# Value-row loads, graph 3's row copies and graph 2's list ranks at other places of the order

## The chip, the cores and the metric

One core of a Trainium2 chip runs the whole program. The metric is the device time of one launch in microseconds (us). The kernel before took 1257.94 us, median of 3 runs (1255.73 to 1259.4).

## What is computed

Eight graphs of 1024 nodes with 128 features, and an adjacency matrix of 1024 x 1024 each (about 8 neighbours a row), go through two layers with residuals:

```python
h = jnp.maximum(_layernorm(x, axis=-1), 0.0)
x = x + _L0_gnn_ref(adj, h, L0_gnn_W, L0_gnn_b)
h = jnp.maximum(_layernorm(x, axis=-1), 0.0)
x = x + _L1_gnn_ref(h, adj, ...)
```

The first layer takes for each node the first 25 neighbours, the maximum over their feature rows, and a linear layer with ReLU of [node, maximum]. The second is a transformer block with 8 heads of 16: scores masked by adjacency in either direction and the diagonal, softmax, output projection, layer norm, a feed-forward net of 512, layer norm.

## The kernel before, in words

The program is written engine by engine, with semaphores set by hand. Time is cut into slots s = -3 to 8 of 32 steps n (`STEPS`). In slot s, TensorE and ScalarE do the attention of graph g = s: step n is one tile of 128 keys for a group of four heads and one half of the queries (`scores`, L1664 and L1668; `exps`, L1460; `contexts` of the step before, L1684). Steps 0 to 15 take the near half of the queries, 16 to 31 the far half. What belongs to other graphs hangs on numbered steps, by tables at the head of the file: the end of graph p = s - 1 (projection, feed-forward, output), the first layer of graph f = s + 1, the neighbour lists of graph r = s + 2, the adjacency and rows of graph l = s + 3. The three engines TensorE, ScalarE and SP issue strictly in this order; a wait of one instruction holds all behind it.

The pieces that the change and the prediction name:

- Lists. DVE reads the adjacency tiles (`list_tile`, L825 and L829), takes candidates, and `merge_pair` makes 25 keys per node. `find_crowded` (L853, L854) tells whether any block of 128 columns held more than it kept. TensorE turns that vector into a row (L1845, at `full_at` of `RANK_AT`), `crowded_tiles` (L859) reads it, `make_lists` (L881 to L900) counts and signals the matmuls `rank_counts` (L1608 to L1611, at `counts_at`), and `list_ranks` (L906 to L909) makes the ranks. POOL waits for them in `scatter_lists` (L667), reloads the sorted lists (`load_lists`, L660) and then gathers neighbour rows, one indirect DMA for each list position (`gather_tile`, L694), some of them held to a pace of the score steps.
- Maxima. DVE reduces the gathered rows (`pool_tile`, L1015), POOL sends them out sorted back (`send`, L674), SP loads them as `ag`, and TensorE transposes them (L1570, at the first of `aggregate_steps`: 22 for f = 1, 20 for f > 1). ScalarE copies the halves out (L1440), and the linear layer follows (L1565 to L1772).
- Banks. PSUM tile `m` has three banks that all of this shares. `refill(bank)` makes TensorE wait until its last user is done. Bank 2 holds the edge counts of step 20 (`NEAR_AT_1`, entry `20: [(2, 2)]`, matmuls L1593 to L1598), and before them the context rows that step 18 transposed (L1713), until DVE's `context` (L1031, L1034) has normalised them.
- Graph 3's rows. `first_norm` on DVE makes the factors, ScalarE's `first_norm` (L1476) applies them to `xh` in eight copies at steps of `H_AT_1`, SP stores them (`store_h_rows`, L502) and loads graph 4's later.
- Value rows. ScalarE writes them at step 30 (L1497); SP spreads them over `va` in seven pieces per head group (`turn_values`, L485 and L487), of which the contexts of the next slot's first step need those of group 0. SP's `load_list_tile` waits until the buffer's last tile has been read:

```python
if i >= 2:
    sp.wait_ge(s_adj_used, i - 1)
sp.dma_start(adj_t[:, t % 2, :], adj[l, t * P:(t + 1) * P, :]).then_inc(ADJ[t % 2], 16)
```

The DVE order in slot 0, written out by hand in `first_slot`, has at the place in question:

```python
find_crowded()
merge_pair(6)
wide_maxima(0, 1)
context(0, 1)
crowded_tiles(2)
make_lists(2)
list_ranks(2)
join_first(1)
first_norm(3)
linear(1)
```

Of the kernel before, what the change touches and what calls it, by code (L numbers as in the profile page):

```python
# [64 lines left out]
NEAR_AT_1 = {17: [(0, 2), (1, 0)], 20: [(2, 2)], 21: [(3, 2)], 23: [(4, 2)], 24: [(5, 2)], 25: [(6, 2)], 31: [(7, 2)]}  # L65
H_AT = {17: (0, 2), 19: (2, 4), 21: (4, 5), 22: (5, 8)}
H_AT_1 = {22: (0, 4), 23: (4, 8)}

CTXT_AT, EARLY_CTXT_AT = [{3}, {3}], {20}
OUTPROJ_AT, EARLY_OUTPROJ_AT = [{4}, {5}], {21}  # L70
# [16 lines left out]

RANK_AT = {0: (-2, 3, 7, 8), 1: (0, 0, 2, 4), 2: (0, 19, 21, None), 3: (1, 11, 12, None)}  # L90


def rank_bank(r):
# [14 lines left out]
def masks_at(s):  # L108

    return MASK_AT_FRONT.get(s, {}) if s < 0 else (MASK_AT_0, MASK_AT_1, MASK_AT)[min(s, 2)]  # L110
# [7 lines left out]
def rank_steps(r):  # L118

    return RANK_AT.get(r, (r - 2, 3, 7, None))  # L120

# [67 lines left out]
def program(nc, x, adj, L0_W, L0_b, Wqkv, bqkv, Wo, bo, ln1_g, ln1_b, W1, b1, W2, b2, ln2_g, ln2_b, out):  # L189
# [6 lines left out]
    with ctx:  # L196
# [199 lines left out]
        def live(g):  # L396
            return 0 <= g < B
# [55 lines left out]
        with nc.Block() as block:  # L453

            @block.sync
            def _(sp):

                def load_list_tile(l, t):
                    i = l * T + t
# [4 lines that stand above are left out]
                def load_shift(g, qh):  # L464

                    sp.wait_ge(s_nflag, g + 1)
                    wide = sp.value_load(nflag_i[0:1, g % 2:g % 2 + 1], min_val=0, max_val=1)
                    with sp.If(wide > 0):
                        sp.wait_ge(s_gshift, 4 * g + 2 * qh + 2)
                        for h in range(HEADS):  # L470
                            q = queries_of(h // GROUP, g, qh)
                            at = h % GROUP * SPAN + (D - first_row(h) % SPAN)
                            sp.dma_start(q[at:at + 1, :], shf[h * TH:(h + 1) * TH, :]).then_inc(s_shift_in, 16)
                    with sp.Else():
                        sp.sem_inc(s_shift_in, 16 * HEADS)

                def turn_values(f, hg):

                    sp.wait_ge(s_v_sb, 2 * f + 2)
                    if f:  # L480
                        sp.wait_ge(s_pv, STEPS * f - (0 if hg else T))
                    for a in range(GROUP):
                        at = a * SPAN
                        h = hg * GROUP + a
                        sp.dma_start(va[0:P - at, hg, a, :, :], v_rows[at:P, h, :, :]).then_inc(VA[hg], 16)  # L485
                        if a:
                            sp.dma_start(va[P - at:P, hg, a, :, :], v_rows[0:at, h, :, :]).then_inc(VA[hg], 16)  # L487
# [10 lines left out]
                def store_h_rows(l):  # L498
                    sp.wait_ge(s_h_ready, T * (l + 1))
                    if l == 0:  # L500
                        sp.wait_ge(s_h_rows_out, 16)
                    sp.dma_start(rows_of(table(l)), xh[:, :, :]).then_inc(s_h_rows_out, 16)  # L502

                def load_x1_half(f, h):

                    k = slice(h * TH, (h + 1) * TH)
                    sp.dma_start(x1[:, f % 2, k, :], graph(x, f)[:, k, :]).then_inc(s_x1_in, 16)

                def load_x(l):
                    if l:  # L510
                        sp.wait_ge(s_h_rows_out, 16 * (l + 1))
                    sp.dma_start(xh[:, :, :], graph(x, l)).then_inc(s_x_in, 16)

                def load_h(f):
                    if f:
                        sp.wait_ge(s_hT_ready, 2 * f)
                    else:
                        sp.wait_ge(s_h_rows_out, 32)
                    sp.dma_start(hl[:, :, :], rows_of(table(f))).then_inc(s_hl_in, 16)

                def load_pooled(f):
                    sent(f + 1)
                    sp.wait_ge(s_aT_ready, 2 * f)
                    sp.dma_start(ag[:, :, :], rows_of(pooled[f % 2])).then_inc(s_ag_in, 16)
# [24 lines left out]
                def first_slot():  # L549
                    load_shift(0, 0)  # L550
                    turn_values(0, 1)
                    load_list_tile(2, 2)
                    load_list_tile(2, 3)
                    store_h_rows(2)
                    load_list_tile(2, 4)
                    load_h(1)
                    load_list_tile(2, 5)
                    load_x1_half(1, 0)
                    load_list_tile(2, 6)
                    load_x1_half(1, 1)  # L560
                    load_list_tile(2, 7)
                    load_x(3)
                    load_list_tile(3, 0)
                    load_list_tile(3, 1)
                    load_pooled(1)
                    load_shift(0, 1)
                    store_h_rows(3)
                    for t in range(2, 6):
                        load_list_tile(3, t)
                    turn_values(1, 0)  # L570

                prologue()
                first_slot()
                for s in range(1, B + 1):
                    g, p, f, r, l = s, s - 1, s + 1, s + 2, s + 3
# [820 lines left out]
            def _(act):  # L1396
# [109 lines left out]
                for s in range(-3, B + 1):  # L1506
                    g, p, f, r, l = s, s - 1, s + 1, s + 2, s + 3
                    for n in range(STEPS):
                        if live(g):
                            exps(g, n)  # L1510
                        if n == 0 and live(p):
                            context_out(p, 3)
                        if n in (8, 16, 24) and live(g):
                            context_out(g, n // T - 1)
                        if live(g):
                            for kt, bank in (FAR_AT if g else FAR_AT_0).get(n, ()):
                                bar(g, kt, bank, 1, s_far_counts, s_far_ready)
                        for e, h, _ in closing(s, n, CTXT_AT, EARLY_CTXT_AT):
                            half_out(turned[:, h * HALF:(h + 1) * HALF], h, s_ctxT_ready, 2 * e + h + 1, s_ctxT_sb)
                        for e, h, _ in closing(s, n, NT_AT, EARLY_NT_AT):  # L1520
                            norm_out(e, h)
                        for e, h, at in closing(s, n, HID_AT, EARLY_HID_AT):
                            for k, bank in at[n]:
                                hidden(e, h * FC + k, bank)
                        for ahead, t in masks_at(s).get(n, ()):
                            if live(s + ahead):
                                mask_tile(s + ahead, t)
                        if s == -2 and n == 10:
                            for kt, bank in NEAR_0:
                                bar(0, kt, bank, 0, s_near_counts, s_near_ready)  # L1530
                        if s == 0 and n in (7, 8):
                            for t in range((n - 7) * TH, (n - 6) * TH):
                                first_norm(2, t)
                        if live(l) and l not in (0, 2):
                            for t in range(*(H_AT if l > 4 else H_AT_1).get(n, (0, 0))):
                                first_norm(l, t)
                        if live(f):
                            if n in (18, 19) if f else n in (3, 4):
                                h = n - (18 if f else 3)
                                half_out(hT[:, h * HALF:(h + 1) * HALF], 0, s_hT_ready, 2 * f + h + 1, s_hT_sb)  # L1540
                            for kt, bank in near_at(f).get(n, ()):
                                bar(f, kt, bank, 0, s_near_counts, s_near_ready)
                            if n == aggregate_steps(f)[0]:
                                halves_out(aT, f, s_aT_ready, s_aT_sb)
                            if n == aggregate_steps(f)[2]:
                                if p >= 0:

                                    act.wait_ge(s_out_stored, 32 * (p + 1))
                                halves_out(h2T, f, s_h2T_ready, s_h2T_sb, ACT.Relu)
                            if n == 30:  # L1550
                                value_rows(f, 0)
                                value_rows(f, 1)
                            for j, bank in projections_at(f).get(n, ()):
                                projection(f, j, bank)
# [367 lines left out]
```

## Time and profile before

| | |
|---|---|
| median of 3 runs | 1257.94 us (1255.73 to 1259.4) |
| profiled execution, its own time | 1255.8 us |
| its span | 1253.8 us, 29308 instructions |
| granted TensorE clock, mean | 0.943 |
| busy: TensorE, DVE, ScalarE, POOL | 83%, 64%, 64%, 59% |

Times in the rows are microseconds from the start of the span. L numbers are lines of the kernel before. A row of a timeline gives start, duration, engine, line, operation, out<-in, shapes and count; in brackets stands how long the engine was idle before it, and what ended that. Slot 0 runs from about 160 to 295 us, slot 1 to 458.

### The profile page before, as it was taken

The numbers are of one execution on the slowest core, as the hardware profiler recorded it, in microseconds if no ns is written. First come the engines' busy times: TensorE is split into PE (matmuls) and PEld (weight loads), VectorE is DVE, ScalarE is ACT, GpSimd is POOL, SyncE is SP. The second block draws the span as 40 slices with busy tenths as digits, with TensorE's granted clock in tenths as the row PEclk, the third lists the DMA queues.
The fourth block names the chain that finished last, engine by engine and source line by source line (L and its number), as shares of the span: only waits on it lengthen the run. The fifth ranks groups of instructions, "written<-read, shape, count | busy, mean of one in ns | idle before, by whom it ended". The sixth has DMA issues, their size and how long they took to land.

```text
span 1253.8 us, 29308 instructions
## 1 busy us (share of the span) xinstructions
PE 1043.9 (83%) x11014; PEld 405.0 (32%) x11014; DVE 797.5 (64%) x3053; ACT 805.7 (64%) x1031; POOL 737.4 (59%) x741
## 2 busy tenths in 40 slices
PE   0125587688984989999999999999999999999874
PEld 0112331233331334343434333433343334333222
DVE  7856877767788477977797769776363534122323
ACT  1321257677852867788778877887678756875541
POOL 4776677567777777777777777776777520000000
PEclk9567889899996999999999999999999999999996
DMA  6533336426423433453345334431242110000000
GB/s 188 167 67 107 104 94 160 145 70 140 119 67 113 110 111 106 123 105 104 110 127 105 100 114 126 104 93 52 80 70 71 53 52 18 21 1 10 10 9 8
DMA packets 95156, 110.77 MB, mean 88 GB/s; under 512 B 17080, under 2 KB 75968, under 8 KB 94976
## 3 DMA queue, kind: packets, MB, share of 16 engines
q1 hardware_dynamic: 68352, 62.67, 16.4%
q0 software_dynamic: 22816, 44.61, 15.5%
q8 instruction: 101, 1.65, 0.6%
q10 hardware_dynamic: 3808, 1.19, 0.4%
q14 instruction: 79, 0.65, 0.2%
HBM read 91.10 MB, written 12.85 MB: 83 GB/s over the span
## 4 chain that ended last, share of the span: by engine, by line
PE 64%; ACT 11%; DVE 7%; POOL 7%; issue 6%; DMA 3%; SPq 0%; DVEq 0%; POOLq 0%; ACTq 0%
PE sc L1664 20%; PE cb L1684 13%; ACT probs L1460 10%; PE sc L1668 7%; PE m L1741 5%; PE m L1749 5%; POOL nb_low L716 3%; PE m L1570 3%; POOL nb_low L694 2%; PE m L1593 2%; DMA nb_low<-h_rows,lsorted 1%; PE m L1723 1%; PE m L1598 1%; PE m L1792 1%; PE m L1771 1%
## 5 line engine op out<-in xcount | busy, mean ns | idle before, releaser
L1460 ACT ACTIVATE probs<-sc 128x1024 f32<-128x1024 f32 x512 | 496.7, 1023 | 245.8 <-PE sc L1668 242.4
L694 POOL DMA_INDIRECT nb_low<-h_rows,lsorted x474 | 470.3, 992 | 168.8 <-issue 129.1
L1684 PE MATMUL cb<-probs,va 128*17 128x512 f32 x2048 | 270.6, 600 | 4.1 <-issue 3.2
L1664 PE MATMUL sc<-q_near,k_g 32*128 32x512 f32 x1024 | 147.8, 647 | 21.4 <-ACT probs L1460 17.2
L1664 PE MATMUL sc<-q_far,k_g 32*128 32x512 f32 x1024 | 149.6, 654 | 16.9 <-ACT probs L1460 15.8
L1015 DVE TENSOR_REDUCE agg<-nb_low 128x128 f32<-128x1024 f32 (+10 forms) x58 | 96.3, 1660 | 60.2 <-DMA nb_low<-h_rows,lsorted 34.4
L1668 PE MATMUL sc<-barred,negident 32*32 32x512 bf16 x4096 | 112.5, 386 | 1.8 <-issue 1.8
L829 DVE MAX8 cand<-keys 128x8 f16<-128x128 f16 x512 | 105.3, 278 | 2.2
L716 POOL DMA_INDIRECT nb_low<-h_rows,first_lists x80 | 80.5, 1006 | 41.9 <-issue 22.5
L1668 PEld LDWEIGHTS sc<-barred,negident 32*32 32x32 bf16 x4096 | 35.4, 88 | 200.8 <-issue 200.8
L1452 ACT ACTIVATE barred<-m 128x512 bf16<-128x512 f32 x128 | 72.9, 608 | 39.5 <-PE m L1598 39.5
L1471 ACT ACTIVATE m<-keys 128x1024 fp8e5<-128x1024 f16 x64 | 67.1, 1058 | 38.3 <-DVE keys L825 38.3
L825 DVE SCALAR_TENSOR_TENSOR keys<-adj_t,prio 128x1024 f16<-128x1024 int32 x64 | 79.0, 1234 | 10.5 <-DVEq L1022 7.7
L674 POOL DMA_INDIRECT pooled_rows<-agg,lsorted x56 | 60.6, 1082 | 26.4 <-issue 14.6
L667 POOL DMA_INDIRECT neighbour_lists<-lst,rank_i x48 | 49.5, 1031 | 28.8 <-DVE rank_i L909 15.3
L1741 PE MATMUL m<-turned,w1T 128*128 128x512 f32 x128 | 65.2, 634 | 1.0 <-ACT turned L1444 1.0
L1749 PE MATMUL m<-wide_tiles,w2T 128*128 128x512 f32 x128 | 63.2, 617 | 0.0
L1664 PEld LDWEIGHTS sc<-q_near,k_g 32*128 32x128 f32 x1024 | 40.4, 184 | 70.4 <-ACT probs L1460 43.6
L1664 PEld LDWEIGHTS sc<-q_far,k_g 32*128 32x128 f32 x1024 | 40.8, 186 | 65.0 <-ACT probs L1460 44.3
L694 POOL DMA_INDIRECT nb_high<-h_rows,lsorted x46 | 46.5, 1011 | 14.0 <-issue 12.8
L1684 PEld LDWEIGHTS cb<-probs,va 128*17 128x17 f32 x2048 | 34.1, 95 | 62.6 <-issue 61.9
L1484 ACT ACTIVATE wide_tiles<-m,b1c 128x512 f32<-128x512 f32 x64 | 44.0, 687 | 15.2 <-PE m L1741 13.7
(180 smaller groups left out, 1442.2 us busy)
## 6 DMA issues: line engine op xcount, KB each, us to landing
adj_t<-in_adj_dram SPq DMA_DIRECT2D x64, 512.0 KB
nb_low<-h_rows,lsorted POOLq DMA_INDIRECT x474
xh<-in_x_dram SPq DMA_DIRECT2D x8, 512.0 KB
h_rows<-xh SPq DMA_DIRECT2D x8, 512.0 KB
hl<-h_rows SPq DMA_DIRECT2D x8, 512.0 KB
x<-in_x_dram SPq DMA_DIRECT2D x16, 256.0 KB
out_dram<-h2T SPq DMA_DIRECT2D x16, 256.0 KB, 3.2
ag<-pooled_rows SPq DMA_DIRECT2D x7, 512.0 KB
```

What stands on the lines that cost most here:

```text
L694: pool.indirect_dma_start(out=dst, out_offset=None, in_=h_rows[0:(f + 1) * (N + 1), :], in_offset=bass.IndirectOffsetOnAxis(ap=lsorted[:, ...
L716: pool.indirect_dma_start(out=first_slots(t)[:, k, :], out_offset=None, in_=h_rows[0:(f + 1) * (N + 1), :], in_offset=bass.IndirectOffsetO ...
L825: nc.vector.scalar_tensor_tensor(out=keys[:, t, :], in0=adj_t[:, t % 2, :], scalar=0.0, in1=prio[:, :], op0=ALU.not_equal, op1=ALU.mult).t ...
L829: ch.step(nc.vector.max(cand[:, t, 8 * c:8 * c + 8], keys[:, t, c * CW:(c + 1) * CW]))
L1015: ch.link(nc.vector.tensor_reduce(a, first.rearrange("p k c -> p c k"), AX.X, ALU.max))
L1452: nc.scalar.activation(barred[:, kt, half * HALF:(half + 1) * HALF], m[:, bank, :], ACT.Relu, bias=1.0, scale=-1.0).then_inc(done, 1)
L1460: nc.scalar.activation(probs[:, i % 2, 2 * pair:2 * pair + 2, :], sc[:, 2 * pair:2 * pair + 2, :], ACT.Exp, scale=SCALE).then_inc(s_probs, 1)
L1664: nc.tensor.matmul(sc[:, a, :], k[part, :], q[part, :], start=True, stop=False)
L1668: last = nc.tensor.matmul(sc[c * SPAN:(c + 1) * SPAN, a, :], negident[b, b], barred[b, kt, qh * HALF:(qh + 1) * HALF], start=False, stop=True)
L1684: last = nc.tensor.matmul(cb[a * SPAN:a * SPAN + VW, :], va[:, u % 2, a, kt, :], probs[:, i % 2, a, :], start=(kt == 0), stop=(kt == T - 1))
L1741: nc.tensor.matmul(m[:, bank, :], w1T[:, k * P:(k + 1) * P], turned[:, half * HALF:(half + 1) * HALF], start=True, stop=True).then_inc(s_h ...
L1749: last = nc.tensor.matmul(m[:, half, :], w2T[:, k, :], hid[:, k, :], start=(k == 0), stop=(k == FC - 1))
```

## The change

Three edits of order; no operation is added or removed, and no semaphore count changes.

```diff
+H_AT_3 = {24: (0, 4), 25: (4, 8)}
...
-RANK_AT = {0: (-2, 3, 7, 8), 1: (0, 0, 2, 4), 2: (0, 19, 21, None), 3: (1, 11, 12, None)}
+RANK_AT = {0: (-2, 3, 7, 8), 1: (0, 0, 2, 4), 2: (0, 21, 22, None), 3: (1, 11, 12, None)}
...
-                    for t in range(2, 6):
+                    for t in range(2, 5):
                         load_list_tile(3, t)
                     turn_values(1, 0)
+                    load_list_tile(3, 5)
...
-                            for t in range(*(H_AT if l > 4 else H_AT_1).get(n, (0, 0))):
+                            for t in range(*(H_AT if l > 4 else H_AT_3 if l == 3 else H_AT_1).get(n, (0, 0))):
                                 first_norm(l, t)
```

The numbers of `RANK_AT` are slot, step of the crowded-rows transpose, step of the counts, step of the sort. Graph 3 is l in slot 0 alone, so all three edits act in slot 0. `H_AT_1` has steps 22 and 23 for these rows.

TensorE's order, from the head transposes of step 18 (`hl`) to the start of the counts, before:

```order
L1570 MATMUL m<-identf,hl 128x128 x4
L1664 MATMUL sc<-q_far,k_g 128x512 x4
L1668 MATMUL sc<-barred,negident 32x512 x16
L1684 MATMUL cb<-probs,va 17x512 x4
L1845 MATMUL m<-identf,full 1x128
L1570 MATMUL m<-identf,hl 128x128 x4
L1664 MATMUL sc<-q_far,k_g 128x512 x4
L1668 MATMUL sc<-barred,negident 32x512 x16
L1684 MATMUL cb<-probs,va 17x512 x4
L1593 MATMUL m<-m,ident 128x512
L1596 MATMUL m<-ident 128x128
L1598 MATMUL m<-ident,m 128x128 x4
```

The same place now (all lines are two further down), to the crowded-rows transpose of step 21:

```order
L1572 MATMUL m<-identf,hl 128x128 x4
L1666 MATMUL sc<-q_far,k_g 128x512 x4
L1670 MATMUL sc<-barred,negident 32x512 x16
L1686 MATMUL cb<-probs,va 17x512 x4
L1595 MATMUL m<-m,ident 128x512
L1598 MATMUL m<-ident 128x128
L1600 MATMUL m<-ident,m 128x128 x4
L1666 MATMUL sc<-q_far,k_g 128x512 x4
L1670 MATMUL sc<-barred,negident 32x512 x16
L1686 MATMUL cb<-probs,va 17x512 x4
L1847 MATMUL m<-identf,full 1x128
```

The first row here is the transposes of step 19. The crowded-rows transpose stood ahead of them; it now stands behind the edge count of step 20 (the L1595 row) and the scores and contexts of step 21. The counts, which stood behind step 21's contexts, stand behind step 22's.

## Rows read from the trace of the kernel before

**Rows 1.** The page: the chain that ended last, shares of the span by engine

```profile
PE 64%; ACT 11%; DVE 7%; POOL 7%; issue 6%; DMA 3%; SPq 0%; DVEq 0%; POOLq 0%; ACTq 0%
```

**Rows 2.** Windows: us; busy (x count) of PE, PEld, DVE, ACT, POOL; clock; DMA; GB/s

```profile
160.00:295.00 135.00, 110.52 (x1378) 41.25 (x1378) 100.59 (x419) 95.57 (x125) 92.49 (x89) 0.95 0.42 116
295.00:458.00 163.00, 131.57 (x1363) 50.29 (x1363) 119.26 (x445) 102.60 (x132) 124.62 (x124) 0.92 0.40 108
458.00:585.00 127.00, 124.24 (x1375) 47.92 (x1371) 97.45 (x371) 100.28 (x128) 96.95 (x95) 1.00 0.42 111
...
241.40:246.00 4.60, 4.56 (x38) 1.63 (x38) 3.21 (x24) 1.45 (x2) 0.68 (x1) 0.64 0.10 35
```

**Rows 3.** Timeline of PE in slot 0, steps 19 to 24

```profile
232.00 1.14 PE L1664 MATMUL sc<-q_far,k_g 32*128 32x512 f32 x8 [0.23 <-ACT probs L1460]
...
241.44 0.37 PE L1845 MATMUL m<-identf,full 128*1 128x128 f32 x1 [6.95 <-DVE full L854]
...
242.60 2.09 PE L1664 MATMUL sc<-q_far,k_g 32*128 32x512 f32 x8
...
245.99 0.39 PE L1593 MATMUL m<-m,ident 128*128 128x512 fp8e5 x1
...
247.14 1.14 PE L1664 MATMUL sc<-q_far,k_g 32*128 32x512 f32 x8 [0.48 <-ACT probs L1460]
...
249.56 0.19 PE L1608 MATMUL m<-abovesum,onesb 128*128 128x26 bf16 x1
...
260.33 0.39 PE L1565 MATMUL m<-bias_tiles,onesb 128*128 128x512 bf16 x1 [2.49 <-ACT wide_tiles L1440]
```

**Rows 4.** Timeline of DVE in slot 0, context rows and lists of graph 2

```profile
245.14 0.42 DVE L1034 TENSOR_TENSOR ctxn<-m,rden 128x256 f32<-128x256 f32 x1
245.48 0.27 DVE L859 TENSOR_REDUCE crowded<-m 1x1 f32<-1x128 f32 x1
...
249.19 0.18 DVE L888 CAST abovesum<-rprod 128x26 bf16<-128x26 f32 x1
```

**Rows 5.** Timeline of ACT in slot 0, steps 19, 22 and 26

```profile
233.55 1.94 ACT L1460 ACTIVATE probs<-sc 128x1024 f32<-128x1024 f32 x2 [1.12 <-PE sc L1668]
...
258.15 1.65 ACT L1476 ACTIVATE xh<-xh,nw 128x128 f32<-128x128 f32 x4 [3.40 <-DVE nw L790]
...
272.69 1.94 ACT L1460 ACTIVATE probs<-sc 128x1024 f32<-128x1024 f32 x2 [0.17 <-PE sc L1668]
```

**Rows 6.** Timeline of POOL, first scatter and first gather of graph 2

```profile
252.12 1.18 POOL L667 DMA_INDIRECT neighbour_lists<-lst,rank_i  x1 [10.04 <-DVE rank_i L909]
...
271.02 1.01 POOL L694 DMA_INDIRECT nb_low<-h_rows,lsorted  x1 [4.28 <-issue]
```

**Rows 7.** Waits of POOL, 271 to 393 us: total us, times, longest us

```profile
POOL nb_low L694 <- issue: 22.4, 61, 4.3
```

**Rows 8.** Timeline of DVE and of PE in slot 1

```profile
344.58 2.13 DVE L1015 TENSOR_REDUCE agg<-nb_low 128x128 f32<-128x1152 f32 x1 [2.97 <-DMA nb_low<-h_rows,lsorted]
...
348.32 0.27 PE L1845 MATMUL m<-identf,full 128*1 128x128 f32 x1 [2.01 <-DVE ctxn L1034]
...
348.63 0.28 DVE L859 TENSOR_REDUCE crowded<-m 1x1 f32<-1x128 f32 x1 [0.45 <-PE m L1845]
...
351.98 0.18 DVE L888 CAST abovesum<-rprod 128x26 bf16<-128x26 f32 x1
...
383.99 1.12 PE L1757 MATMUL m<-identf,turned 128*128 128x128 f32 x4 [9.19 <-DVE turned L1054]
...
405.09 1.97 PE L1570 MATMUL m<-identf,ag 128*128 128x128 f32 x8 [9.21 <-DMA ag<-pooled_rows]
```

**Rows 9.** Timeline of SP and of PE at the border to slot 1

```profile
276.85 16.71 SPq L462 DMA_DIRECT2D adj_t<-in_adj_dram  x4
293.66 1.21 SPq L485 DMA_DIRECT2D va<-v_rows  x2
...
303.43 1.91 PE L1684 MATMUL cb<-probs,va 128*17 128x512 f32 x8 [3.23 <-issue]
```

## The prediction

> **What bounds the kernel now.** I read the page's chain of waits first: it runs through TensorE for 64% of the span, with DVE and POOL at 7% each [rows 1]. The sum of busy times by stage says where to look [rows 2]: the third (458 to 585 us, the pattern of the later ones) takes about 127 us, TensorE 98% busy at the full clock of 2.4 GHz, while the first takes 135 us and the second 163 us, with POOL busy for 124.6 us of that. All three edits act in slot 0 and on the border to slot 1, so the question is what ends the waits there.
>
> Slot 0 first, on TensorE [rows 3]. Step 19 starts at 232.00. In it TensorE stands 6.95 us for the crowded-rows vector of graph 2, until 241.44 [rows 3]. Right after, the step's score matmuls take 2.09 instead of 1.14 us, and the stretch from 241.4 to 246.0 has a granted clock of 0.64 [rows 2]: most of it ran at 1.2 GHz, after an idle time of 7 us. The second stand, 2.49 us at 260.33, is for the copy of the pooled rows, which ScalarE runs behind the row copies of graph 3, and these wait 3.40 us for DVE's norm [rows 5].
>
> POOL next. It stands 10.04 us for graph 2's ranks, scatters the lists at 252.12, reloads them and gathers from 271.02 [rows 6]. From there to 371 us no gather waits more than 0.3 us, save the first: POOL is issue-bound for 100 us [rows 7]. What waits for it is slot 1: DVE waits 2.97 us for a gather until 344.58, TensorE then 2.01, 9.19 and 9.21 us, for DVE work behind those gathers and for the pooled rows [rows 8]. **So slot 1 is set by the moment at which the ranks of graph 2 are ready,** not by TensorE. After 458 us only TensorE and ScalarE are on the chain; a shift that stands there stays to the end.
>
> **Crowded rows and counts, from steps 19 and 21 to 21 and 22.** What the edit wants is the 6.95 us: steps 19 and 20 could run first. Step 19 needs 2.42 us from its first score to the end of its contexts (247.14 to 249.56), then half a microsecond of transposes; ScalarE ends its exponentials at 235.5 (233.55 and 1.94) [rows 5], step 20 starts there and is through at 238.0. But the next instruction in step 20 is the edge count of tile 2, in bank 2, which holds the context rows of step 18 until DVE has normalised them. DVE does that at 245.14 to 245.56 [rows 4], behind the crowded-rows reduction and a merge of lists, and nothing in its queue since the transposes of step 18 waits for TensorE. Before, the count began at 245.99 and waited for nothing. Now it begins at 245.6. **The stand moves from step 19 to step 20 and lasts 7.6 us; of 6.95 us some 0.4 us is won.**
>
> From there the new places cost. Step 21's scores and contexts now stand ahead of the crowded-rows transpose, and they run just behind a stand as long as that of before, so I take step 20's own times of before for them: 3.39 us from score to end of contexts (242.60 to 245.99), and about 1.0 us for the edge count in place of 0.6. Thus: count 245.6, step 21 at 246.6, transpose at 250.0. DVE takes it 0.31 us later, as at 348.32 and 348.63 in slot 1 [rows 8], and needs from there to the vector for the counts 3.53 us (348.63 to 352.16; where DVE came late to it, 245.48 to 249.37 [rows 4], it was 3.89). That gives 253.9, and step 22's contexts are through at 253.6 (exponentials of step 21 end at 251.1, plus 2.42). The counts start at 254.0 instead of 249.56: **+4.4 us**. With the full clock the same sum is 246.2, 248.6, 248.9, 252.5, counts at 252.7: +3.1 us, the lower end. With 3.89 in place of 3.53 it is +4.8. Behind the counts everything up to POOL is a fixed chain of 2.56 us (249.56 to 252.12), and from the first scatter to the first gather 18.9 us: scatter at 256.5, first gather at 275.4. POOL is past its pacing there (the first gather needs only step 24's scores), so nothing gives these back.
>
> On the clock, the Trainium skill, "TensorE: Matmul & The Clock Gate", section "What's actually happening", says that for modelling the ramp is under 1% of a typical span and that one should not fit a count of slow matmuls; by that the 1.3 us between my two sums would be left out and the result be the +3.1. The row of step 20, 2.09 against 1.14 us, speaks for keeping it.
>
> **Row copies of graph 3, from steps 22 and 23 to 24 and 25.** Removed: ScalarE's wait of 3.40 us for DVE's norm and 1.65 us of copies ahead of the pooled rows' copy, so TensorE's 2.49 us. But the join of graph 1, behind the ranks in DVE's queue, is now 4.4 us later too, and step 22's transposes wait for it. Of these 4.4 us the 2.49 and about 1 us of slack ahead of the transposes are taken off again, so I put step 24 about 1 us behind before. Added: 1.65 us in each of steps 24 and 25, and ScalarE has only 0.17 us idle at the end of step 25 [rows 5], which makes 1.5 us there; in step 24 the linear layer's matmuls hide a part, and I take half, 0.8 us (together 2.3, between 1.5 and 3.3). Together TensorE enters slot 1 some 3 us later. SP's store of these rows waits for the last of them, at the end of step 25, about 275 us by my estimate (step 26's exponentials, before at 272.69, stand behind them); the next tile load behind it was issued at 276.85 [rows 9] when its buffer came free, so a cover of 1 to 2 us stays, more with DVE late.
>
> **Value rows ahead of tile 5.** Before, SP's four tile loads end at 293.56, the last held by DVE's keys, and the seven pieces follow from 293.66 at 0.6 us or more each [rows 9]; TensorE stands 3.23 us for the last of them and does the contexts in 1.91 us [rows 9], about half of it at the full clock by my estimate: 3.23 and 0.9 make 4.1 us to be had. Now they are issued as soon as the value rows are written (some 3 us later than before, by the shift above) and no 512 KB tile is ahead of them. I take all of it as removed. Tile 5 is issued some 5 us later; DVE needs it behind the first tile of graph 2 and the tile before, over 10 us later than it was issued, so a part of that is left.
>
> **What comes of the sum.** TensorE is then about 1 us ahead of before at step 2 of slot 1 (+3 less 4.1). But the gathers are 4.4 us later: DVE's 344.58 becomes 349.0, TensorE's 348.32 becomes 352.7, and so on with 383.99 and 405.09. Gains on TensorE ahead of these only lengthen the stands. So copies and value rows are worth nothing now; what hides them is TensorE's own wait for the gathers. If that cover were gone they would be worth about 1 us together. The sum is +4.4 us on the profiled execution, 1255.8 us, which lies 2.1 us under the median of the runs: 1260.2 against it, **1262.3 us** against the median of 1257.94. A measurement of this kernel can tell about 0.3%, 3.8 us, from no change, so this is just beyond.
>
> **Rivals.** (a) The delay is real but smaller: full clock for step 21, +3.1 us, 1261.0, or a gather that lands sooner behind other loads. For it: the clock may return at another point of the step. Against: the rows after the stands at 241.44 and 303.43 are both slow. 22%. (b) The edit does not reach the path: context rows and ranks come so that the counts are ready by 249.6 to 251, POOL starts as before, and slot 1 hides all else: 1257.9. Against: bank 2 is free at 245.56 only. 12%. (c) **Faster:** slot 1 is not held by the gathers but by TensorE, that is, the landing at 344.58 has over 4.4 us of slack. It decides from the point where gathers land before DVE asks. Then the 3.23 us and the slow contexts (4.1 us) and the 2.49 us come through, less 2.3 us on ScalarE: -4.3 us, 1253.6. Against: DVE waits 2.97 us there and TensorE 20 us after it [rows 8]. 6%. (d) More than the sum: the longer stands of slot 1 (3 us and more at step 8, before the norm's transposes) bring the low clock into the feed-forward matmuls, whose results DVE needs; each such stretch costs 1 to 2 us: 1264 to 1267. 10%. The forecast has 50%.
>
> **Numbers.** The range reaches from (b) to the lower half of (d): 1257.0 to 1266.0. Beyond 1261.7 is slower by over 0.3%: the forecast's upper part, (d) and a third of (a), 0.58. Within: the rest of the forecast, most of (a), (b), 0.35. Faster: (c) and a little noise, 0.07.
>
> **What would show it.** In the new profile: no wait for the crowded rows in step 19, but an idle time of about 7.6 us on the edge count of step 20, ended by the context rows at 245.6; slow scores in step 21; counts at 254; first scatter at 256.5, first gather of graph 2 at 275.4; no wait of the step-1 contexts for the value rows; no wait for the pooled rows' copy at 260; DVE's wait for the gather ended at about 349, the transposes of the sum at 388.4, the pooled rows at 409.5; slots from the third on at 126 us. I am wrong if the scatter starts before 254, or if it starts at 256 and 405.09 has not moved with it.

## The result

The changed kernel takes **1263.54 us** (median of 13 runs, 1260.47 to 1265.26); the kernel before, in the same sessions, 1259.4 us (13 runs, 1255.67 to 1261.97). The ratio is 1.0035, 95% interval 1.0023 to 1.0047: 4.1 us slower between the medians, where +4.4 was the sum and 1262.3 the forecast (counted from the 1257.94 us of the first three runs).

The profiled execution of the change has a span of 1262.0 us, 8.2 more than the one before. Not all of this is the change's: DVE's context rows in slot 0, which no edit touches, end at 248.76 in place of 245.56. So 3.2 us lie ahead of the edits (2.1 of them already at the scores of step 18), and I compare distances from that point. Timeline of the change, TensorE in slot 0 and 1 (lines are two further down than in [rows 3] and [rows 8]):

```profile
248.91 0.59 PE L1595 MATMUL m<-m,ident 128*128 128x512 fp8e5 x1 [8.82 <-DVE ctxn L1036]
249.96 2.09 PE L1666 MATMUL sc<-q_far,k_g 32*128 32x512 f32 x8
...
253.33 0.27 PE L1847 MATMUL m<-identf,full 128*1 128x128 f32 x1
...
254.46 1.14 PE L1666 MATMUL sc<-q_far,k_g 32*128 32x512 f32 x8 [0.36 <-ACT probs L1462]
...
257.66 0.17 PE L1610 MATMUL m<-abovesum,onesb 128*128 128x26 bf16 x1 [0.72 <-DVE abovesum L890]
...
261.79 1.71 PE L1666 MATMUL sc<-q_far,k_g 32*128 32x512 f32 x8
...
266.23 0.38 PE L1567 MATMUL m<-bias_tiles,onesb 128*128 128x512 bf16 x1
...
308.99 1.05 PE L1686 MATMUL cb<-probs,va 128*17 128x512 f32 x8
...
357.74 0.34 PE L1847 MATMUL m<-identf,full 128*1 128x128 f32 x1 [2.06 <-DVE ctxn L1036]
...
393.43 1.11 PE L1759 MATMUL m<-identf,turned 128*128 128x128 f32 x4 [7.70 <-DVE turned L1056]
...
414.91 1.33 PE L1572 MATMUL m<-identf,ag 128*128 128x128 f32 x5 [8.99 <-DMA ag<-pooled_rows]
```

The stand of 6.95 us for the crowded rows [rows 3] is gone, and one of 8.82 us stands on the edge count of step 20, ended by DVE's context rows. The counts begin 8.9 us after these rows' end (257.66 less 248.76); before it was 4.0. The two small waits that the other edits aim at are gone: nothing is waited for at 266.23 (before 2.49 us) or at 308.99 (before 3.23 us [rows 9]). The waits of slot 1 are all there.

DVE in the same kernel, the timeline of its context rows, the crowded-rows reduction, the vector for the counts, and its wait for a gather in slot 1:

```profile
248.34 0.42 DVE L1036 TENSOR_TENSOR ctxn<-m,rden 128x256 f32<-128x256 f32 x1
...
253.64 0.28 DVE L861 TENSOR_REDUCE crowded<-m 1x1 f32<-1x128 f32 x1 [4.87 <-PE m L1847]
...
257.33 0.18 DVE L890 CAST abovesum<-rprod 128x26 bf16<-128x26 f32 x1
...
354.00 2.13 DVE L1017 TENSOR_REDUCE agg<-nb_low 128x128 f32<-128x1152 f32 x1 [2.73 <-DMA nb_low<-h_rows,lsorted]
```

POOL, the same timeline view, answers to [rows 6]:

```profile
260.22 1.17 POOL L669 DMA_INDIRECT neighbour_lists<-lst,rank_i  x1 [14.92 <-DVE rank_i L911]
...
275.42 0.95 POOL L662 DMA_DIRECT2D lsorted<-neighbour_lists  x1 [2.73 <-issue]
...
280.04 1.01 POOL L696 DMA_INDIRECT nb_low<-h_rows,lsorted  x1 [3.67 <-issue]
```

The first scatter waits 14.92 us for the ranks, 4.9 more. Less the 3.2 us, the first gather is 5.8 us late. The waits of slot 1 end at 354.00, 357.74, 393.43 and 414.91, 6.2, 6.2, 6.2 and 6.6 us late, where the forecast had 4.4 for all of them; at the end of the span it is 5.0. By stage (windows; columns as in [rows 2]), the third slot is what it was, 126.5 us against 127.0. The last line is the stretch behind the stand, with a granted clock of 0.66:

```profile
304.00:468.50 164.50, 134.21 (x1363) 49.99 (x1359) 120.08 (x446) 102.67 (x131) 125.89 (x124) 0.91 0.39 108
468.50:595.00 126.50, 124.99 (x1383) 48.08 (x1379) 96.80 (x370) 100.40 (x129) 96.50 (x94) 1.00 0.41 109
248.90:253.40 4.50, 4.49 (x39) 1.44 (x40) 0.00 (x0) 1.53 (x3) 0.00 (x0) 0.66 0.27 80
```

### The profile page after: what moved, and what is told of

It is laid out like the page before. It is cut to its first block, busy times and chain, and to the rows that moved or that the text cites. A ratio compares the mean times of both kernels' runs of the same rounds, so it can differ in the third digit from the quotient of the medians.

```text
span 1262.0 us, 29308 instructions
## 1 busy us (share of the span) xinstructions
PE 1055.2 (84%) x11014; PEld 407.7 (32%) x11014; DVE 797.9 (63%) x3053; ACT 806.4 (64%) x1031; POOL 736.5 (58%) x741
## 3 DMA queue, kind: packets, MB, share of 16 engines
q0 software_dynamic: 22816, 44.61, 15.4%
## 4 chain that ended last, share of the span: by engine, by line
PE 61%; DVE 12%; ACT 9%; POOL 6%; issue 6%; DMA 5%; DVEq 1%; SPq 0%; POOLq 0%; ACTq 0%
PE sc L1666 18%; PE cb L1686 13%; ACT probs L1462 7%; PE sc L1670 6%; PE m L1743 4%; PE m L1751 4%; POOL nb_low L718 3%; DMA nb_low<-h_rows,lsorted 3%; PE m L1572 3%; POOL nb_low L696 2%; DVE agg L1017 2%; PE m L1595 2%; PE sc L1708 2%; PE m L1600 1%; DVE st L769 1%
## 5 line engine op out<-in xcount | busy, mean ns | idle before, releaser
L1686 PE MATMUL cb<-probs,va 128*17 128x512 f32 x2048 | 273.5, 606 | 2.2 <-DMA va<-v_rows 1.6
L1670 PEld LDWEIGHTS sc<-barred,negident 32*32 32x32 bf16 x4096 | 35.4, 88 | 200.5 <-issue 200.5
L1595 PE MATMUL m<-m,ident 128*128 128x512 fp8e5 x128 | 52.2, 408 | 9.7 <-DVE ctxn L1036 8.8
```

Of the source, the lines that this page charges most:

```text
L1595: nc.tensor.matmul(o, ident8[:, :], m1[:, f % GRAPHS, kt, half * HALF:(half + 1) * HALF], start=True, stop=False)
L1670: last = nc.tensor.matmul(sc[c * SPAN:(c + 1) * SPAN, a, :], negident[b, b], barred[b, kt, qh * HALF:(qh + 1) * HALF], start=False, stop=True)
L1686: last = nc.tensor.matmul(cb[a * SPAN:a * SPAN + VW, :], va[:, u % 2, a, kt, :], probs[:, i % 2, a, :], start=(kt == 0), stop=(kt == T - 1))
```

## The experiments

Two theories stand against each other: slot 1 is held by the gathers, so the moment of graph 2's ranks decides; or it is held by TensorE, so what TensorE wins or loses in slot 0 decides. All ratios are to the kernel before, with 95% intervals, 12 runs of each kernel against 17 to 35 of the kernel before.

**1. The rank edit alone.**

```diff
-RANK_AT = {..., 2: (0, 19, 21, None), ...}
+RANK_AT = {..., 2: (0, 21, 22, None), ...}
```

> Only the crowded-rows transpose and the counts of graph 2 are moved (steps 21 and 22). Theory (ranks late, slot 1 held by the gathers): all of the 4.1 us is here, ratio 1.003 to 1.004; TensorE stands 7 to 9 us on the edge count of step 20 until DVE has normalised the context rows, the counts start 4 to 5 us later against the end of that normalisation than before (4.0 us after it before, 8.8 in the change), the first scatter likewise. Rival (the row copies of steps 24 and 25 do it, 2 to 3 us of ScalarE, and the ranks little): ratio under 1.0015.

Measured: 1.0029 (1.0017 to 1.0041), 1263.49 us. Within the intervals it is the whole loss. Its timeline of TensorE (two lines up from the change's numbers):

```profile
248.68 0.58 PE L1593 MATMUL m<-m,ident 128*128 128x512 fp8e5 x1 [8.57 <-DVE ctxn L1034]
...
258.60 0.17 PE L1608 MATMUL m<-abovesum,onesb 128*128 128x26 bf16 x1 [0.85 <-DVE abovesum L888]
```

And a window of the same kernel, with the columns of [rows 2]:

```profile
245.00:255.00 10.00, 6.32 (x43) 1.91 (x44) 2.64 (x19) 2.54 (x3) 0.05 (x1) 0.50 0.21 60
```

The counts start 10.1 us after the context rows, later than in the whole change and than the 8 to 9 expected; the granted clock was 0.50 for all of the ten microseconds, and step 21's contexts took 1.91 us, where in the change it had risen before these contexts (1.05 us).

**2. The change without the rank edit,** measured twice.

> The change without its rank edit: row copies in steps 24 and 25 and value rows ahead of tile 5, ranks in steps 19 and 21 as before. Theory: TensorE is 2 to 4 us ahead in slot 1 at steps 2 to 8 and stands that much longer for the gathers afterwards; ratio 0.999 to 1.001. Rival (slot 1 held by TensorE): the gain stays to the end, 3 to 4 us, ratio 0.997.

Measured: 0.9984 (0.9970 to 0.9999). TensorE reached step 2 of slot 1 after 7.2 us from step 0 in place of 11.5, and stood longer later. The upper end was close enough to 1 to ask again:

> The change without its rank edit once more, since the first measurement had its upper end at 0.9999. Theory (nothing to be had while the gathers hold slot 1): 0.999 to 1.0005, with the first gather 981 to 984 us ahead of the end. Rival (row copies and value rows are worth 2 us after all): 0.997 to 0.9985.

Measured: 1.0009 (0.9992 to 1.0025). The same kernel lies 0.0025 apart in two sessions. So there is no gain to show, and a single ratio here is good to some 0.001 to 0.002 whatever its interval.

**3. Row copies alone, value rows alone.**

> Only graph 3's row copies are moved to steps 24 and 25. Theory: the wait of 2.5 us for the pooled rows' copy in step 23 goes, 2 to 3 us of ScalarE come back in steps 24 and 25, TensorE enters slot 1 within 1 us of before, the ranks are as before, ratio 0.999 to 1.001. Rival (ScalarE's added work reaches the end): ratio 1.002.

Measured: 0.9988 (0.9974 to 1.0003). TensorE's wait for the pooled rows' copy was gone and it entered slot 1 at the same distance, 24.1 us, after the first gather as before.

> Only the value rows of slot 1 are loaded ahead of tile 5. Theory: the 3.2 us stand of slot 1's step 1 is gone, step 2 comes 11.5 us less 3.5 to 4.1 after step 0, TensorE stands as much longer for the gathers later, first gather to end 983 us as before, ratio 0.999 to 1.001. Rival (slot 1 held by TensorE): ratio 0.997.

Measured: 1.0002 (0.9984 to 1.0019). The time is as both the first theory and no effect would have it, but the edit did not do its work: step 2 came 11.3 us after step 0. SyncE's queue, from the timeline of this kernel, has the issue of tile 5:

```profile
299.70 0.58 SPq L462 DMA_DIRECT2D adj_t<-in_adj_dram  x1
```

And TensorE in the same kernel has the first contexts that read the value rows:

```profile
304.71 1.91 PE L1685 MATMUL cb<-probs,va 128*17 128x512 f32 x8 [2.88 <-ACT probs L1461]
```

Tile 5 is issued at 299.70, behind the pieces, which went out as soon as the value rows were written (293.8), yet the contexts still stood 2.88 us. From the end of the value rows to the contexts it took 10.9 us, against 11.2 before, and 8.1 to 9.8 in all runs that have both edits. My reading, that tile 5 ahead of them was the whole of the wait, fails; with both edits the stand is gone or at most 1.8 us. Why the pieces land sooner with both edits was not tried.

**4. The bank.** The edge count of step 20 in bank 1, beside the whole change:

```diff
-NEAR_AT_1 = {17: [(0, 2), (1, 0)], 20: [(2, 2)], 21: [(3, 2)], ...}
+NEAR_AT_1 = {17: [(0, 2), (1, 0)], 20: [(2, 1)], 21: [(3, 2)], ...}
```

> The whole change, and in addition the edge count of tile 2 in step 20 uses bank 1 in place of bank 2, so that it need not wait for the context rows. Theory (the bank is what makes the rank edit harmful): TensorE does steps 19 and 20 and the crowded-rows transpose of step 21 without a stand, waits then for the context rows at the edge count of step 21, and the counts start 4.0 to 4.6 us after the end of the context rows' normalisation in place of 8.8: time as before, ratio 0.999 to 1.001. Rival (two steps more ahead of the counts are what delays them, whatever the bank): ratio 1.003 as in the change.

Measured: 1.0005 (0.9991 to 1.0019). In the time, one number gives the loss back. TensorE in this kernel's timeline:

```profile
243.53 0.27 PE L1847 MATMUL m<-identf,full 128*1 128x128 f32 x1 [0.98 <-DVE full L856]
247.79 0.59 PE L1595 MATMUL m<-m,ident 128*128 128x512 fp8e5 x1 [4.00 <-DVE ctxn L1036]
248.84 2.09 PE L1666 MATMUL sc<-q_far,k_g 32*128 32x512 f32 x8
...
251.44 1.91 PE L1686 MATMUL cb<-probs,va 128*17 128x512 f32 x8
253.29 0.20 PE L1610 MATMUL m<-abovesum,onesb 128*128 128x26 bf16 x1
```

The transpose of the crowded rows now runs 4.3 us ahead of the edge count, where in the change it ran behind it. The counts start 5.7 us after DVE's context rows (end 247.64), not the 4.0 to 4.6 expected. DVE had the vector at 251.43, but TensorE was in step 21 until 253.3, at the low clock behind its stand of 4.00 us (scores 2.09 us, contexts 1.91 us). So the counts follow step 21 here, not the vector. The first gather is still 2.9 us later against DVE's crowded-rows vector than before (table below), more than the time shows.

**5. POOL alone made late.** The kernel before, with 14 small chained memsets on POOL ahead of the first scatter:

```diff
+                        pool.wait_ge(s_ranks, 2 * (f + 2))
+                        for k in range(14):
+                            pool.memset(delay[:, :], 0.0).then_inc(s_delay, 1)
+                            pool.wait_ge(s_delay, k + 1)
                         scatter_lists(f + 1)
```

> The kernel before, with 14 chained small POOL memsets between the arrival of graph 2's ranks and the first scatter; nothing else moves, TensorE, ScalarE and DVE have slot 0 as before. They should hold POOL 3 to 5 us, to be read from the trace as d. Theory (slot 1 is held by the gathers): the time grows by d, within 1 us, ratio about 1.003 for 4 us, and step 0 of slot 1 stays where it was. Rival (the gathers have slack): ratio under 1.001.

Measured: 1.0035 (1.0021 to 1.0050). TensorE entered slot 1 at the same distance from DVE's crowded-rows vector as before (54.0 us against 53.8), and the kernel was as slow as the change. POOL:

```profile
253.41 2.86 POOL L749 MEMSET delay<- 128x64 f32 x14 [10.00 <-DVE rank_i L915]
256.86 0.97 POOL L669 DMA_INDIRECT neighbour_lists<-lst,rank_i  x1 [0.58 <-POOL delay L749]
...
273.34 0.95 POOL L662 DMA_DIRECT2D lsorted<-neighbour_lists  x1 [4.22 <-issue]
...
277.63 1.65 POOL L696 DMA_INDIRECT nb_low<-h_rows,lsorted  x1 [3.34 <-issue]
```

The memsets held it 3.45 us; the reload then waited 4.22 us for the scattered rows where it was 1.16 before, and the first gather came 30.7 us after the context rows in place of 25.5.

**6. The stand filled.** The change, with matmuls into the free bank 1 in step 20, ahead of the edge count:

```diff
+                            if s == 0 and n == 20:
+                                refill(1)
+                                for _ in range(30):
+                                    nc.tensor.matmul(m[:, 1, :], onesb[:, :], bias_t[...], start=True, stop=True)
```

> The change, with 30 extra matmuls (128x512, bf16, into bank 1, which is free there) in step 20 ahead of the edge count, that fill TensorE's stand. Theory (step 21 at the low clock costs 1.3 us on the way to the counts): the granted clock stays at 1.0 through step 21, its contexts end 2.4 instead of 3.4 us after its first score, the counts start 7.3 to 7.8 us after the end of the context rows' normalisation instead of 8.9, time 1 us or so under the change, ratio 1.002 to 1.003. Rival (the clock plays no part, ScalarE or DVE sets the counts): counts at 8.9 as in the change.

Measured: 1.0000 (0.9984 to 1.0016), counts at 8.9 us. The fill ended 2.22 us early, and the clock fell all the same, a little later (windows, columns of [rows 2]):

```profile
247.60:249.00 1.40, 1.40 (x14) 0.67 (x14) 0.00 (x0) 0.60 (x1) 0.00 (x0) 0.97 0.95 289
249.00:252.00 3.00, 3.00 (x29) 0.36 (x26) 0.00 (x0) 1.78 (x2) 0.00 (x0) 0.50 0.01 2
```

So as a test of the clock it failed, and its counts are as late as the change's; yet its time is that of before. With 39 in place of 30:

> As the run with 30 extra matmuls, with 39, so that they fill all of the 8.8 us that TensorE stood (30 left 2.2 us, and the clock fell right behind). Theory (step 21 at the low clock costs 1.3 us on the way to the counts): clock 1.0 from step 20 to the counts, which start 7.3 to 7.8 us after the end of the context rows' normalisation instead of 8.9, and the first gather 29.5 to 30 us after it instead of 31.2; time 1 us under the change. Rival (something else sets the counts): 8.9 us as in the change, at the full clock.

Measured: 1.0004 (0.9989 to 1.0019). The fill ran 1.3 us past the context rows, and the counts started 8.6 us after them, 7.3 from the start of the edge count. With 35:

> As the run with 39 extra matmuls, with 35, since 39 ran 1.2 us past the moment at which the context rows were ready, and its time (1.0004) was lower than the sum asks. Theory (the fill gives back the 1.3 us of the low clock and no more): counts 7.4 to 7.7 us after the end of the context rows' normalisation, ratio 1.0020 to 1.0030. Rival (the fill gives back all that the change cost, by something that the profile of one execution does not show): ratio under 1.0012.

Measured: 0.9996 (0.9983 to 1.0010). TensorE in this kernel's timeline:

```profile
239.00 7.73 PE L1870 MATMUL m<-bias_tiles,onesb 128*128 128x512 bf16 x35
247.20 0.38 PE L1595 MATMUL m<-m,ident 128*128 128x512 fp8e5 x1 [0.48 <-DVE ctxn L1036]
247.79 1.14 PE L1666 MATMUL sc<-q_far,k_g 32*128 32x512 f32 x8
...
254.53 0.17 PE L1610 MATMUL m<-abovesum,onesb 128*128 128x26 bf16 x1 [0.72 <-DVE abovesum L890]
```

And its granted clock over the same stretch, a window with the columns of [rows 2]:

```profile
237.00:258.00 21.00, 17.71 (x192) 7.22 (x184) 12.35 (x57) 8.80 (x11) 4.87 (x5) 1.00 0.29 90
```

From the edge count to the counts it is 7.3 us at the full clock, against 8.75 in the change and 9.9 in experiment 1. So the low clock was worth 1.4 to 2.6 us on this path. But the rival that I wrote down won: the time is that of before, three times over, though the counts are still 3.5 us later than there. The profile of this run has the first gather 32.6 us after DVE's crowded-rows vector, against 29.6 before and 35.4 in the change: 2.8 of the 5.8 us are given back; with 39 it is 33.6 and with 30 it is 34.0. That the times of the filled runs are some 4 to 5 us under the change's is not accounted for. The clock can't be the reason in all three, since with 30 it was low in step 21. What the extra matmuls change besides was not tried.

**7. Ranks sooner.** Both edge counts off bank 2 (`20: [(2, 1)], 21: [(3, 0)]`), and `context(0, 1)` moved behind `make_lists(2)`, on top of the change:

> The change with the edge counts of steps 20 and 21 in banks 1 and 0, so that none waits for the context rows, and DVE's normalisation of these rows moved behind the lists of graph 2. Theory: TensorE does not stand before the counts of step 22, the vector for the counts is ready about 0.7 us sooner after DVE's crowded-rows reduction than before (8.0 us there, 7.3 now), the first scatter 0 to 1 us sooner than before against the same point (10.7 us there), and slot 1 follows it: ratio 0.998 to 1.0. Rival (slot 1 held by TensorE): the two steps won show in full, ratio under 0.996.

Measured: 1.0002 (0.9987 to 1.0017). The first scatter came 10.1 us after DVE's crowded-rows vector (10.7 before), and TensorE stood 3.52 us ahead of the counts, where I expected no stand: the two steps that it wins buy nothing. A gain of 0.7 us is under what the runs can tell. Going further, the last two tiles of graph 1 pooled behind the lists:

> As the run with the context rows behind the lists, and in addition the last two tiles of graph 1 are pooled by DVE behind the lists of graph 2 instead of ahead of the crowded-rows reduction. Theory: the first scatter comes about 2 us sooner than before, the pooled rows of graph 1 and so the join 3 to 5 us later, which TensorE can bear; slot 1 follows the scatter, ratio 0.997 to 0.999. Rival (the late join holds slot 0's end and from there the rest): ratio 1.001 or more.

Measured: 1.0009 (0.9994 to 1.0023). No gain, and the reason is in POOL's queue:

```profile
254.23 0.98 POOL L676 DMA_INDIRECT pooled_rows<-agg,lsorted  x1 [11.65 <-DVEq L1026]
255.67 0.97 POOL L676 DMA_INDIRECT pooled_rows<-agg,lsorted  x1 [0.45 <-DVEq L1026]
257.36 0.96 POOL L669 DMA_INDIRECT neighbour_lists<-lst,rank_i  x1 [0.73 <-DVE rank_i L911]
```

The sends of those tiles stand ahead of the scatters and now wait for the pooling, so the scatter was not sooner at all (11.9 us after DVE's vector). No version beat the kernel before beyond what the two sessions of experiment 2 lie apart.

**All runs together.** The times are in us, from one profiled execution of each kernel: the first gather of graph 2; how far it lies behind the end of DVE's crowded-rows vector; from the gather to the end of the span; TensorE's first score of step 0 of slot 1, counted from the gather. The ratio is that of all runs, as above.

| kernel | first gather | behind the vector | to the end | step 0 of slot 1 | ratio |
|---|---|---|---|---|---|
| before | 271.0 | 29.6 | 982.8 | +24.1 | 1 |
| change | 280.0 | 35.4 | 982.0 | +23.8 | 1.0035 |
| ranks alone | 280.2 | 35.8 | 983.3 | +24.0 | 1.0029 |
| without ranks, twice | 270.4, 273.9 | 30.2, 31.0 | 983.1, 981.5 | +22.3, +23.5 | 0.9984, 1.0009 |
| copies alone | 270.6 | 30.4 | 982.4 | +24.1 | 0.9988 |
| value rows alone | 272.9 | 30.3 | 981.8 | +23.9 | 1.0002 |
| bank | 276.0 | 32.5 | 981.1 | +23.5 | 1.0005 |
| POOL late | 277.6 | 34.9 | 982.7 | +19.1 | 1.0035 |
| filled, 30, 39, 35 | 277.2, 277.7, 275.5 | 34.0, 33.6, 32.6 | 981.4, 980.9, 981.8 | +23.6, +26.3, +23.7 | 1.0000, 1.0004, 0.9996 |
| context behind lists | 274.6 | 28.3 | 983.2 | +24.3 | 1.0002 |
| lists first | 277.5 | 32.0 | 981.8 | +27.2 | 1.0009 |

The end follows the gather within 2.4 us in fourteen executions, while TensorE's entry into slot 1 moves by 8 us against it. Part of the gather's own movement lies ahead of the edits (the vector itself ends between 240.2 and 246.4), and would leave the distance to the end alone under either theory; what tells them apart is the rows in which TensorE's entry moved against the gather, POOL late above all. This is the link that the prediction rested on, and with experiment 5 its direction is shown.

Its size is not. The three kernels with the gather 34.9 us or more behind the vector lose 0.29% to 0.35%; but the bank and the three filled ones have it 2.9 to 4.3 us later than before, and lose 0.05% (0.6 us) at most, with intervals that end at 0.10% to 0.19%. One profiled execution stands for each kernel, and it can lie 2 to 4 us from the median: the kernel before's took 1255.8 us against a median of 1259.4, that with 30 extra matmuls 1260.29 against 1257.57. Whether that is all, or the gathers have some play up to about 4 us, no run here decides.

## Why the prediction was right

- **The stand moves to step 20.** Right: 8.82 us on the edge count, forecast 7.6; experiment 4 shows that the bank is its cause, since with bank 1 nothing is waited for there.
- **Counts 4.4 us later.** Measured +4.9 in the profile. Step 21 took 3.4 us at the low clock as forecast; the term mis-sized is DVE's time from the crowded rows to the vector, 3.53 us in the sum, 3.87 here (253.64 to 257.51), which I had only as the upper end.
- **Scatter to gather 18.9 us.** 19.8 in the change; the reload waited 2.73 in place of 1.16. With it the gather is 5.8 us late in the profile, not 4.4.
- **The time.** The medians say 4.1 us, the profiles 5.0 at the end and 6.2 to 6.6 in slot 1. So the chain of causes held, but that the sum of 4.4 lies within 0.3 us of the medians is in part luck: two of its terms were too short by some 1.3 us together, and the end was less late than the gather.
- **Low clock kept in the sum.** Right for the counts: 8.75 us from the edge count in the change, 7.3 at the full clock. The Trainium skill, "TensorE: Matmul & The Clock Gate", section "What's actually happening", advises to leave the ramp out as under 1% of a span. The trace agrees with the figure, 1.4 to 2.6 us of some 1260; but it stood on the path. In the time it is not shown, since the filled run with the low clock (1.0000) lies where the two at the full clock do (1.0004, 0.9996).
- **Copies and value rows worth nothing under the gathers.** Right in time. Wrong in three sizes: TensorE entered slot 1 5.4 us late against the context rows (8.6 less 3.2), not 3, and the clock was low in step 23 again (scores 1.71 us); at step 2 it was 1.1 us behind (310.96 against 306.68, less 3.2), not 1 ahead; and the value-row edit alone does not remove the wait.
- **Rivals.** (a) asked for the full clock in step 21; the change had 0.66 over that stretch, and with the full clock the counts come at +3.5, but the time did not follow. (c), TensorE as the bound, fell with experiments 2 and 5. (b) was not seen: the counts were late. Of (d) the trace has the mechanism but not the price: behind stands of 2.42 and 2.06 us in slot 1 the scores took 2.06 and 2.09 us (at 340.65 and 358.01), where before they took 1.14; copies alone had such a step too (2.09 at 348.96) and lost nothing.

## What to carry to other kernels

Before an order is changed to skip a wait, go down the waiting engine's own queue to the next instruction that needs something, banks included: here it waited for the same engine's next result, 4 us later. And an instruction moved behind that stand carries everything it feeds with it; on the path was not the engine with the idle time but POOL, four handovers on. Where one queue is saturated for a whole stage, the start of that queue is the number to watch; how much of its delay reaches the end has to be measured.

## What was not expected of the hardware

The low clock after a stand lasted differently long in like executions: 0.66 on average over the 4.5 us behind it in the change, 0.50 for all of 245 to 255 us with the rank edit alone. With 30 extra matmuls in the stand, 6.65 of 8.87 us, it still fell, about 1.3 us after TensorE had gone on (0.97 from 247.6 to 249.0, then 0.50). From the first scatter to the reload of the lists it took 13.6 to 15.4 us in the runs where POOL was not held, with the same eight scatters at the same pace; 15.2 in the change, 13.7 before and with the rank edit alone. What decides it stays open.
